# The recurrence's gathered rows: the first group summed in step two, the later ones weighed by two engines and added by TensorE

## The reference

```python
x = x + layernorm(attention0(layernorm(x)))
x = x + layernorm(experts0(layernorm(x)))      # 32 experts, top 4
x = x + layernorm(rwkv(layernorm(x)))          # the stage of this change
x = x + layernorm(experts1(layernorm(x)))
```

```python
ww = time_first + kk;  p = max(pp, ww)
e1 = exp(pp - p);      e2 = exp(ww - p)
out = (e1 * aa + e2 * vv) / (e1 * bb + e2)
ww2 = pp + w;          p2 = max(ww2, kk)
e1b = exp(ww2 - p2);   e2b = exp(kk - p2)
carry = (e1b * aa + e2b * vv, e1b * bb + e2b, p2)
```

## Time and profile before

| | |
|---|---|
| time, median of 3 runs | 1125.14 us (1124.09 to 1128.04) |
| the profiled execution: time | 1130.16 us |
| the profiled execution: span of the core | 1128.4 us |
| mean granted TensorE clock | 0.866 |
| busy over the span: PE, DVE, ACT, POOL | 871.4, 741.7, 640.1, 537.1 us |

### The profile page before, as it was taken

The page is one execution under the profiler, slowest core; times in us unless marked ns, Lnnn a source line. Parts: engine busy times, 40 slices in busy tenths (PEclk is TensorE's granted clock), DMA queues, the critical chain, the costliest instruction groups (busy, mean ns, idle before and its releaser), DMA issues. The chain is left out here.

```text
span 1128.4 us, 19649 instructions
## 1 busy us (share of the span) xinstructions
PE 871.4 (77%) x5836; PEld 701.8 (62%) x5836; DVE 741.7 (66%) x2333; ACT 640.1 (57%) x1330; POOL 537.1 (48%) x689
## 2 busy tenths in 40 slices
PE   3897667666549988998996637677757799999993
PEld 2633455555437877997996214344445698999991
DVE  5569688888878565411668599998886944223734
ACT  4253877766554333664665657677676564555551
POOL 0001555568635777774773777000001375777550
PEclk9998687777758999998999768888886799999997
DMA  7999000000071115665774111000003433234214
GB/s 196 290 188 52 1 1 0 0 0 0 1 259 43 51 52 165 200 175 166 200 195 129 50 44 48 7 1 1 0 1 109 176 109 102 83 91 140 80 37 153
DMA packets 146757, 101.43 MB, mean 90 GB/s; under 512 B 22257, under 2 KB 138353, under 8 KB 145649
## 3 DMA queue, kind: packets, MB, share of 16 engines
q1 hardware_dynamic: 133872, 74.10, 25.6%
q0 software_dynamic: 12800, 26.31, 7.7%
HBM read 45.69 MB, written 50.48 MB: 85 GB/s over the span
## 5 line engine op out<-in xcount | busy, mean ns | idle before, releaser
L1278 POOL DMA_INDIRECT e_xs<-h_tok,rows_of x128 | 125.5, 981 | 60.5 <-issue 37.5
L798 ACT ACTIVATE mask<-ps_q,k_neg 128x256 bf16<-128x256 f32 x256 | 100.9, 488 | 28.7 <-PE ps_q L936 28.7
L936 PE MATMUL ps_q<-q_parts,pick 128*128 (+1 forms) x256 | 59.8, 369 | 52.2 <-DVE mask L677 36.8
L1321 POOL DMA_INDIRECT e_ys_tok<-e_y_rows,e_out_ids x80 | 78.5, 982 | 42.2 <-ACT e_y_rows L1658 22.5
L1445 PE MATMUL e_ps_gu<-e_w_all,e_x_turned 128*128 x384 | 94.0, 389 | 0.2 <-issue 0.2
L1988 DVE TENSOR_TENSOR e_hidden<-e_ps_gu,e_hidden 128x512 f32<-128x512 f32 x48 | 33.2, 691 | 89.9 <-ACT e_hidden L1631 89.8
L2008 DVE COPY e_w_here<-e_w_all 128x512 f32 x80 | 34.7, 436 | 83.7 <-PE e_ps_up L1477 80.3
L1278 POOL DMA_INDIRECT e_xs<-e_h_ids,e_rows_of x64 | 63.0, 984 | 49.7 <-DVEq L1829 30.4
L1477 PE MATMUL e_ps_up<-e_x_turned,e_w_here 128*128 128x128 f32 x640 | 85.8, 278 | 0.8 <-ACT e_x_turned L1625 0.8
L2535 POOL DMA_INDIRECT c_got<-e_ys,rows_of x64 | 70.0, 1094 | 33.3 <-issue 19.2
L936 PEld LDWEIGHTS ps_q<-q_parts,pick 128*128 128x128 f32 x256 | 45.4, 247 | 59.7 <-issue 36.5
(11 more groups left out here) (433 smaller groups left out, 2471.6 us busy)
## 6 DMA issues: line engine op xcount, KB each, us to landing
e_xs<-zeros SPq DMA_DIRECT2D x2, 6144.0 KB, 34.4
e_x_rows<-e_xs SPq DMA_DIRECT2D x48, 256.0 KB, 3.1
e_ys<-e_y_rows SPq DMA_DIRECT2D x48, 256.0 KB, 2.4
e_w_all<-in_w SPq DMA_DIRECT2D x4, 1536.0 KB, 12.9
e_x_rows<-e_xs SPq DMA_DIRECT2D x20, 260.0 KB, 3.0
e_xs<-zeros SPq DMA_DIRECT2D x2, 2560.0 KB, 40.6
e_h_ids<-h_tok SPq DMA_DIRECT2D x16, 256.0 KB, 3.7
e_w_all<-in_w SPq DMA_DIRECT2D x4, 1024.0 KB
```

Of the source, the lines that this page charges most:

```text
L798: last = nc.scalar.activation(mask[u][QS // 2 + j][keys][:, h * T:(h + 1) * T], psq[1][:, h * T:(h + 1) * T], ACT.Sign, bias=k_neg[u][:, k ...
L936: last = nc.tensor.matmul(psq[0 if on_dve else 1][:, h * T:(h + 1) * T], pick[:, (quad * HQ + h) * P:(quad * HQ + h + 1) * P], q_parts[:, ...
L1278: nc.gpsimd.indirect_dma_start(out=xs[part], out_offset=bass.IndirectOffsetOnAxis(ap=rows_of[:, j:j + 1], axis=0), in_=rows, in_offset=Non ...
L1321: nc.gpsimd.indirect_dma_start(out=ys_tok, out_offset=bass.IndirectOffsetOnAxis(ap=out_ids[:, i:i + 1], axis=0), in_=tile(y_rows[q % YB], ...
```

## The change

- The first gathered group is no longer summed at the end of step 0 but in step 1, after `peaks(1)` (`first_rows`). Its root (`tail_root(0)`) runs beside `attended(0)`, its `tail_normed` stands at the end of ScalarE's step 1, and its `tail_added` in step 2.
- In step 0 ScalarE does `exps(0)` before `rows_in(1)`.
- For gathered groups 1 to 3 VectorE adds two of the four rows (`half_rows`, 8 instructions). ScalarE multiplies the other two by their weights, in place (`parts_weighed`, 8 instructions of 128 x 128). TensorE adds up `y_tok` and the eight weighted rows in the bank `ps_o` by products with the identity (`tail_sums`: one product of 128 x 512 and eight of 128 x 128). The statistics and `tail_normed` of these groups read the bank.
- `half_rows(1)` stands at the end of VectorE's step 1, `half_rows(2)` and `(3)` behind `peaks` of their steps. `parts_weighed(1)` stands at the end of ScalarE's step 1, the others between `feed` and `exps`. `tail_sums(1)` is at the end of TensorE's step 1, the others follow `feed_out`.
- New waits: `tail_root` of groups 1 to 3 begins with a wait for `tail_ps`, which `tail_sums` signals; `tail_sums` waits for `o_sb`, `parts_added` and `parts_scaled`; `attention_out` 1 to 3 waits for `t_normed`. GpSimd waits for `combined` once and then for `tail_ps`.
- The small tensors of the tail (`t_stats` and the like) are doubled.

```diff
--- before.py
+++ after.py
@@ -2121,11 +2121,12 @@
         GPP, PT, GB = GROUPS // 2, TILES // 2, 2 * TPG
         rows_of0, weight0 = env["rows_of0"], env["weight0"]
         got = [tb(f"got{i}", K0 * P) for i in range(GB)]
-        t_stats = tb("t_stats", TPG * 6)
-        t_mv, t_rstd, t_var, t_shift = tb("t_mv", TPG * 2), tb("t_rstd", TPG), tb("t_var", TPG), tb("t_shift", TPG)
-        t_tmp = tb("t_tmp", TPG)
+        t_stats, t_mv = pair("t_stats", TPG * 6), pair("t_mv", TPG * 2)
+        t_rstd, t_var, t_shift, t_tmp = (pair(n, TPG) for n in ("t_rstd", "t_var", "t_shift", "t_tmp"))
         gathered = [env["plain_semaphore"](f"c_gathered{i}") for i in range(GB)]
         combined, tail_own, t_scaled, t_normed = map(sem, ("combined", "tail_own", "t_scaled", "t_normed"))
+        parts_scaled, parts_added, tail_ps = map(sem, ("parts_scaled", "parts_added", "tail_ps"))
+        ADDS = K0 // 2
         shared2, rests_made, weights_made = map(sem, ("shared2", "rests_made", "weights_made"))
         FEEDS = ("cm_k", "cm_r")
         loaded, derived, chain0, scaled1 = map(sem, ("loaded", "derived", "chain0", "scaled1"))
@@ -2303,11 +2304,11 @@

                 ct = Chain(dve, tail_own)

-                def gathered_in(j):
+                def gathered_in(j, adds):
                     g = GPP + j
                     for t in range(g * TPG, (g + 1) * TPG):
                         dve.wait_ge(gathered[t % GB], 16 * K0 * ((t - PT) // GB + 1))
-                    for k in range(K0):
+                    for k in range(adds):
                         for t in range(g * TPG, (g + 1) * TPG):
                             y = y_tok[:, t * P:(t + 1) * P]
                             if k:
@@ -2317,14 +2318,25 @@
                                                                  ALU.mult, ALU.add)
                             ct.mark(ins)
                     ct.wait()
-                    dve.sem_inc(combined, TPG)
-                    env["group_stats"](ct, group(y_tok, g), t_stats)
+
+                def first_rows():
+                    gathered_in(0, K0)
+                    dve.sem_inc(combined, 1)
+
+                def half_rows(j):
+                    gathered_in(j, ADDS)
+                    dve.sem_inc(parts_added, 1)

                 def tail_root(j):
+                    u = j % 2
+                    if j:
+                        dve.wait_ge(tail_ps, FROM + j)
+                    env["group_stats"](ct, ps_o if j else group(y_tok, GPP), t_stats[u])
+                    yield
                     ct.wait()
-                    yield from env["group_root_steps"](ct, t_stats, t_mv, t_rstd, t_var, t_tmp[:, :])
-                    nc.vector.scalar_tensor_tensor(t_shift[:, :], t_mv[:, :].rearrange("p (t s) -> p t s", s=2)[:, :, 0], -1.0,
-                                                   t_rstd[:, :], ALU.mult, ALU.mult).then_inc(t_scaled, 1)
+                    yield from env["group_root_steps"](ct, t_stats[u], t_mv[u], t_rstd[u], t_var[u], t_tmp[u][:, :])
+                    nc.vector.scalar_tensor_tensor(t_shift[u][:, :], t_mv[u][:, :].rearrange("p (t s) -> p t s", s=2)[:, :, 0],
+                                                   -1.0, t_rstd[u][:, :], ALU.mult, ALU.mult).then_inc(t_scaled, 1)

                 def tail_added(j):
                     g = GPP + j
@@ -2371,7 +2383,9 @@
                             yield

                 def second_stream(n):
-                    if 0 <= n - 1 < GPP:
+                    if n == 2:
+                        yield from tail_added(0)
+                    if 0 < n - 1 < GPP:
                         yield from tail_added(n - 1)
                     if n in (2, 4):
                         yield from row_scales(PT + (n - 2) * TPG, PT + n * TPG)
@@ -2380,7 +2394,7 @@

                 for n in range(GROUPS + 3):
                     now = 0 <= n - 1 < GROUPS
-                    together(output_sums(n - 1) if now else iter(()), tail_root(n - 1) if 0 <= n - 1 < GPP else iter(()),
+                    together(output_sums(n - 1) if now else iter(()), tail_root(n - 1) if 0 < n - 1 < GPP else iter(()),
                              front_y() if n == GROUPS - 1 else iter(()))
                     if n >= 3:
                         product(n - 3)
@@ -2392,12 +2406,16 @@
                         output_ratio(n - 1)
                     if n < GROUPS:
                         peaks(n)
-                    together(attended(n - 1) if now else iter(()), second_stream(n),
+                    if n == 1:
+                        first_rows()
+                    if 1 < n < GPP:
+                        half_rows(n)
+                    together(attended(n - 1) if now else iter(()), second_stream(n), tail_root(0) if n == 1 else iter(()),
                              front_x(0) if n == GROUPS + 1 else iter(()), front_added(2, 3) if n == GROUPS + 1 else iter(()))
                     if n == GROUPS + 1:
                         together(front_x(1))
-                    if n < GPP:
-                        gathered_in(n)
+                    if n == 1:
+                        half_rows(n)
                 dve.wait_ge(stats_done, FROM + TILES)
                 dve.wait_ge(front_ready, FROM + 2)

@@ -2493,9 +2511,20 @@
                     g = GPP + j
                     act.wait_ge(t_scaled, FROM + j + 1)
                     for t in range(TPG):
-                        last = nc.scalar.activation(tile(y_tok, g, t), tile(y_tok, g, t), ACT.Identity,
-                                                    bias=t_shift[:, t:t + 1], scale=t_rstd[:, t:t + 1])
+                        rows = ps_o[:, t * P:(t + 1) * P] if j else tile(y_tok, g, t)
+                        last = nc.scalar.activation(tile(y_tok, g, t), rows, ACT.Identity,
+                                                    bias=t_shift[j % 2][:, t:t + 1], scale=t_rstd[j % 2][:, t:t + 1])
                     last.then_inc(t_normed, 1)
+
+                def parts_weighed(j):
+                    g = GPP + j
+                    for t in range(g * TPG, (g + 1) * TPG):
+                        act.wait_ge(gathered[t % GB], 16 * K0 * ((t - PT) // GB + 1))
+                        for k in range(ADDS, K0):
+                            rows = got[t % GB][:, k * P:(k + 1) * P]
+                            last = nc.scalar.activation(rows, rows, ACT.Identity,
+                                                        scale=weight0[:, k * TILES + t:k * TILES + t + 1])
+                    last.then_inc(parts_scaled, 1)

                 rows_in(0)
                 turned_in(0)
@@ -2503,20 +2532,27 @@
                 for n in range(GROUPS + 2):
                     if n < GROUPS:
                         kvr_in(n)
+                    if n == 0:
+                        exps(n)
                     if n + 1 < GROUPS:
                         rows_in(n + 1)
-                    if 0 <= n - 1 < GPP:
+                    if 0 < n - 1 < GPP:
                         tail_normed(n - 1)
                     if n + 1 < GROUPS:
                         turned_in(n + 1)
                     if n >= 2:
                         feed(n - 2)
-                    if n < GROUPS:
+                    if 1 < n < GPP:
+                        parts_weighed(n)
+                    if 0 < n < GROUPS:
                         exps(n)
                     if 0 <= n - 1 < GROUPS:
                         rows_mid(n - 1)
                         turned_mid(n - 1)
                         shares(n - 1, xc, FEEDS, xc_ready, f_mixed).then_inc(shared2, 1)
+                    if n == 1:
+                        tail_normed(0)
+                        parts_weighed(1)
                     if n == GROUPS - 1:
                         for g in range(GPP - 1):
                             front_norm_y(g)
@@ -2529,8 +2565,10 @@
             @block.gpsimd
             def _(pool):
                 for t in range(PT, TILES):
-                    if t - PT >= GB:
-                        pool.wait_ge(combined, FROM + ((t - PT - GB) // TPG + 1) * TPG)
+                    if t == PT + GB:
+                        pool.wait_ge(combined, FROM + 1)
+                    if t - PT >= GB + TPG:
+                        pool.wait_ge(tail_ps, FROM + (t - PT - GB) // TPG)
                     for k in range(K0):
                         nc.gpsimd.indirect_dma_start(
                             out=got[t % GB][:, k * P:(k + 1) * P], out_offset=None, in_=env["ys0"],
@@ -2559,10 +2597,25 @@
                 def attention_out(g):
                     pe.wait_ge(wkv_ready, FROM + g + 1)
                     pe.wait_ge(o_sb, FROM + g)
+                    if 0 < g < GPP:
+                        pe.wait_ge(t_normed, FROM + g + 1)
                     for t in range(TPG):
                         o = slice(t * P, (t + 1) * P)
                         last = nc.tensor.matmul(ps_o[:, o], wkv[g % 2][:, o], mats["att_Wo"][:, :], start=True, stop=True)
```

(20 more changed lines are left out.)

## The result

| | before | changed |
|---|---|---|
| time, median | 1127.61 us (20 runs, 1123.68 to 1132.71) | 1134.45 us (20 runs, 1127.80 to 1137.33) |
| ratio, 95% interval | | 1.005 (1.0034 to 1.0065), or 5.6 us more (3.8 to 7.3) |
| the profiled execution: time, span | 1130.16, 1128.4 us | 1136.22, 1134.5 us |
| busy: PE, DVE, ACT | 871.4, 741.7, 640.1 us | 877.7, 733.2, 645.7 us |

The change makes the kernel slower by half a per cent. The time forecast was 1128.7, 3.6 above the median known then; measured are 5.6 by the ratio, and 1134.45 lies inside the range, at its upper end. Of the 5.75 us between 1134.45 and 1128.7, 2.47 are the median of the kernel before itself, which was 1125.14 for the three runs known then and is 1127.61 for twenty.

A forecast was written before the change was run, and what follows sets the result against it. VectorE's order was taken to bound steps 1 to 4, ScalarE's exponentials from step 6. Shifts of 3.4, +0.4, -1.5, +1.0, -2.1, +1.0 and +1.4 made 3.6 us on 1125.14: 1128.7, range 1122 to 1134.5.

The forecast's parts named there:

- A(1): Step 1's first half on VectorE, output sums and roots: starts at 637.5 in place of 644.8, 7.3 us gained.
- the end of the wait: VectorE in step 2, after one scan, waits some 8 us for TensorE's sums of group 1, until 673.4.
- A(3): Step 3's first half on VectorE, output sums and roots: starts 2.3 us late, near 701.0, and is 1.0 longer.
- A(4): Step 4's first half on VectorE: starts 1.2 us late after a new 0.7 wait for exponentials; 1.0 longer.
- attention_out(3): TensorE's output product in step 4: starts near 744.6, behind a late third feed product; VectorE waits about 1.2 us.
- attention_out(0): TensorE's output product in step 1: waits for the late rows, ends near 654.3, 2.07 us at the low clock.
- B(1): Step 1 on VectorE from `attended` to its end: two interleaved chains, taking 5.4 us.
- C: Rival: the step 2 wait doesn't decide; A(2), step 2's first half, starts 8.1 us earlier; 1120.6 us; chance 0.11.
- B: Rival: TensorE at its high clock saves 1.9 us in step 1's sums, up to 0.8 in step 4; 1126.1; chance 0.28.
- D: Rival: gathers land late because VectorE's bursts of sums hold GpSimd's issues; 1132.1 us; chance 0.17.
- The statistics of a PSUM bank: VectorE's statistics read from the bank: charged nothing, up to 0.1 us an instruction for the range.
- a shift that shrinks between step 5 and the stage's end, which I have taken as none: Later steps of the stage: step 5's shift of 3.6 us goes through unchanged to the end.

The follow-up runs named there:

- Group 1 on VectorE: Changed kernel, but VectorE sums all four rows of gathered group 1, with no weighing by ScalarE or adding by TensorE; ratio 0.9997 to the kernel before.
- sums-then-root: Changed kernel with VectorE's step 2 output sums issued ahead of group 1's root and its wait, instead of interleaved; ratio 0.9982 to the kernel before.
- weighed first: Changed kernel with ScalarE weighing group 1 ahead of step 1's middle rows and TensorE summing ahead of their turn; ratios 0.9979 and 0.9960 to the kernel before.
- TensorE kept busy: Changed kernel with the identity product of `y_tok` in group 1's sum done three times, so TensorE works while waiting; ratio 1.0003 to the kernel before.
- second set: The changed kernel itself run once more, unedited, beside the kernel before; ratio 1.0066 (1.0047 to 1.0085).
- late head: Seen in the unedited changed kernel's second trace: TensorE's clock rose later in step 0, so r came 1.5 us later; step 2's mark 65.3 for 63.8.
- split only: Changed kernel with the first group's sum and the exponentials placed as before, groups 1 to 3 still split; ratio 1.0017 to the kernel before.

## Why the prediction was right, and where its size was off

**Steps that stood, within about 0.5 us.** The start of A(1) at 637.5 (forecast 637.5), `attended(0)` at 655.2 (655.2), `rows_mid(0)` at 660.5 (660.6), the gathers' wait before `half_rows(1)` ending at 662.5 (663.0), eight weighings in 2.43 (2.4; 392 ns each for the 399 worked out), eight products in 3.78 (3.8), the end of the wait at 673.2 (673.4), A(3) at 701.1 (701.0), A(4) at 727.2 with 0.57 of waiting (727.5 and 0.7), `attention_out(3)` at 744.7 with 1.38 of VectorE waiting (744.6 and 1.2). The shift at step 5's k mix is 3.1 to 3.7 in the three traces, for the 3.6 forecast. Group 1 on VectorE and sums-then-root show that the wait is the cause and not a mark of it: without it, or with work ahead of it, step 2 comes 4.3 to 5.7 earlier. The weighing's place in ScalarE's queue is a good part of it, by weighed first.

**Steps that came out by luck.** `attention_out(3)` is two errors that cancel: the feed product ahead of it began at 743.8, where the sum had 742.9, and took 0.94 us to the next product, where the sum had 1.8 at the low level. `attention_out(0)` was taken at the low level and to end at 654.3; it ran in 1.06 at the high one and ended at 652.7, and nothing waited for it. The terms listed for B(1) add up to 5.2 and not to 5.4; it took 5.3.

**Rivals.** C is out: the gap is 7.67, over its 3. B is out in step 1, where the products ran at the low level; its price of 1.9 for them was right, by the 1.95 for 3.78 of TensorE kept busy. In step 4 the third feed product ran at the high level (granted clock 1.00), as B had it. D is out as a cause: GpSimd had one long issue in the first group's burst,

```profile
655.19 1.01 POOL L2573 DMA_INDIRECT c_got<-e_ys,rows_of  x1 [0.30 <-issue]
656.50 2.58 POOL L2573 DMA_INDIRECT c_got<-e_ys,rows_of  x1 [0.30 <-issue]
659.39 0.95 POOL L2573 DMA_INDIRECT c_got<-e_ys,rows_of  x1 [0.30 <-issue]
```

but the eight weighings, which begin at 670.22, waited for nothing. The half burst at 665.82 stretched no issue (0.94 each). In weighed first the gathers do come to count (1.22 on ScalarE).

**The statistics of a PSUM bank** were charged nothing, and cost nothing: 280 ns each, against 281 from SBUF in the kernel before and 279 for the first group in the changed one. The Trainium skill, VectorE: DVE Perf Modes, section on the TRN2 errata, would have 65 ns more for each, an estimate from its cycles; the measurement decides, and it shows none. The same table lets ScalarE gain by a PSUM source; with that the rows agree in sign: `tail_normed` takes 449 ns from the bank and 477 from `y_tok`.

**The term that was mis-sized** is the last one, "a shift that shrinks between step 5 and the stage's end, which I have taken as none". I carried step 5's shift to the end of the program as a constant. In the mean of three traces of either kernel the shift is 3.3 at step 5, 2.8 at step 9 and 1.6 at the end of the span, and the runs say 5.6. The column from step 5 to 9 shows too that it is no constant: with the same work these steps take 89 us in some kernels and 85 to 87 in others. VectorE waits for ScalarE there, ScalarE for TensorE's k, v and r, and when these come hangs on TensorE's level. Of the kernel before, ScalarE in step 6:

```profile
779.61 0.60 ACT L2437 ACTIVATE c_k<-c_ps_kvr 128x512 f32<-128x512 f32 x1 [0.98 <-PE c_ps_kvr L2556]
781.27 0.60 ACT L2437 ACTIVATE c_v<-c_ps_kvr 128x512 f32<-128x512 f32 x1 [1.06 <-PE c_ps_kvr L2556]
```

TensorE of the kernel before, from the middle rows of step 5 to the k products of step 6:

```profile
775.45 0.99 PE L2546 MATMUL c_ps_t<-ident,y_tok 128*128 128x128 f32 x4 [3.48 <-ACT y_tok L2468]
776.24 1.92 PE L2555 MATMUL c_ps_kvr<-c_xa,c_now_Wk 128*128 128x512 f32 x2
777.95 1.57 PE L2556 MATMUL c_ps_kvr<-c_xa,c_was_Wk 128*128 128x512 f32 x2
```

and of weighed first, second trace:

```profile
773.27 0.66 PE L2585 MATMUL c_ps_t<-ident,y_tok 128*128 128x128 f32 x4 [3.48 <-ACT y_tok L2486]
773.76 1.02 PE L2594 MATMUL c_ps_kvr<-c_xa,c_now_Wk 128*128 128x512 f32 x2
774.62 1.02 PE L2595 MATMUL c_ps_kvr<-c_xa,c_was_Wk 128*128 128x512 f32 x2
```

After the same 3.48 us of idling the one has lost the high level and the other has kept it; from the start of the transposes to the second k product it is 2.50 against 1.35, and the v products follow at 3.90 against 2.21: 1.7 us in one step. By stretches, from step 5's mark to step 9's, of before, and then of weighed first (columns as in the earlier trace rows; the granted clock is the third number from the end):

```profile
758.80:847.80 89.00, 61.48 (x272) 39.19 (x272) 75.42 (x198) 62.94 (x117) 0.00 (x0) 0.84 0.00 1
```

```profile
757.10:842.20 85.10, 58.00 (x272) 37.26 (x272) 75.34 (x197) 60.69 (x113) 0.00 (x0) 0.88 0.00 1
```

The same 272 records, and 3.5 us more of TensorE's time for them in the first. So up to 4 us can come or go in steps 6 to 9 beyond a change's own shift. That the moment at which TensorE falls idle decides it is read from these rows and not tested; no edit is needed for it, as the changed kernel's second trace has 87.1 for 89.2. For the changed kernel this does not explain its loss: its three traces have 89.2, 87.1 and 89.2, the kernel before 89.0. It can account for last marks that are 1 to 5 us earlier than I expected of the mended kernels, and it may not hold in every execution: their runs gained less than their traces.

**What stays open.** In the traces the stage is 233.7, 232.0 and 233.6 long, mean 233.1, against 230.3: 2.8 more, the stage starts at 617.9 in the mean of either, and what follows step 9's mark is in the changed kernel 1.2 shorter (279.6 against 280.8). The traced executions are thus 1.6 longer in the mean. The runs say 5.6 (3.8 to 7.3), and 1.0066 in the second set. From 2.2 to 5.7 us of the loss are thus in no trace that I have. The changed kernel's three traced executions differ among themselves by 7.7 us, 4.6 of it in the stage's start, 1.7 in the stage and 1.4 behind it, so three of them may have missed the mean of the runs by that much; nothing here tests it. The late head is a candidate, as the kernel before doesn't pay for it, but it is worth 1.5 at most at step 2, and in the one trace that had it 0.4 was left at step 5. The same gap stands elsewhere: split only's stage is 6.3 longer in its trace, and its runs are at 1.0017, so by its runs it loses less than the changed kernel, though its mark at step 5 is 3 us later. TensorE kept busy gains 1.9 by step 5 and loses nothing in its runs. A trace and the runs of one kernel agree here only to some 4 us, and a cause of this size can't be settled by single traces. That the direction was right rests on steps shown; that the measured loss exceeds the forecast by 2 rests on nothing I can name. The range reached up to 1134.5 for rival D and what lies beyond it, and D did not happen; that 1134.45 lies inside by 0.05 is luck.

## What to carry to other kernels

Where an engine's order is fixed and two streams are interleaved, a wait at the head of the second stream is a wait of both: before moving work off the full engine, put the wait behind all that does not need it, and place the helpers' part where their queues are idle. Either mend alone brought the loss down to nothing here; both together gave nothing more, since later steps wait for the helpers too. A head that no longer waits for a transfer starts to follow the next thing behind it, here TensorE's clock in its first products. And a shift worked out over some steps should not be carried unchanged through later steps in which an idling TensorE sets the pace.
